# Five instead of four sets of single-row transfers per head, split between SyncE and ScalarE

## The reference

```python
kv_scores, indices = _pk(x, Wq_pk, pk_keys)          # top 16 of 128 x 128 keys, per token and head
ind = indices + offsets[None, None, :, None]         # a head has its own 16384 rows
k = jnp.einsum('bnhk,bnhkd->bnhd', kv_scores, keys_table[ind])
v = jnp.einsum('bnhk,bnhkd->bnhd', kv_scores, values_table[ind])
sim = jnp.where(causal, jnp.einsum('bihd,bjhd->bhij', q, k), neg)
out = jnp.einsum('bhij,bjhd->bhid', softmax(sim), v)
return out.transpose(0, 2, 1, 3).reshape(b, n, HEADS * DIM) @ Wo
```

## Time and profile before

| What | Value |
|---|---|
| Median of 3 runs | 10074.95 us (10071.83 to 10075.61) |
| Span of the profiled execution | 10059.9 us (its own time is not listed; the median of the runs is 15.05 us longer than the span) |
| POOL busy | 7544.0 us, 75% of the span |
| DVE, PE, ACT busy | 69%, 57%, 31% |
| Chain that ended last | POOL 73%, issue 24% |
| DMA, mean | 109 GB/s |
| Mean granted TensorE clock | 0.748 |

### The profile page before, as it was taken

How to read it: one execution, slowest core, us unless ns; L and a number is a source line. 1 busy time by engine, 2 the same in 40 slices (tenths; PEclk the granted TensorE clock), 3 DMA queues, 4 the chain that set the end, 5 groups by cost and what they waited for, 6 DMA issues and landing times.

```text
span 10059.9 us, 190416 instructions
## 1 busy us (share of the span) xinstructions
PE 5726.9 (57%) x23108; PEld 4551.2 (45%) x23108; DVE 6956.2 (69%) x42844; ACT 3087.9 (31%) x9770; POOL 7544.0 (75%) x7957
## 2 busy tenths in 40 slices
PE   5655555555555555555555555555555555555555
PEld 4544444444444444444444444444444444444444
DVE  8876667666666677676776666767667676666664
ACT  4333233233333333333333333333333332322222
POOL 5777777777777777777777777777777777777776
PEclk7877777777777777777777777777777777777777
DMA  3333343333433334333343333333333333333333
GB/s 109 105 109 109 109 114 109 109 109 109 113 109 109 109 109 113 109 109 109 109 113 109 109 109 109 113 109 109 109 111 111 110 109 109 109 111 109 109 109 100
DMA packets 503669, 1100.92 MB, mean 109 GB/s; under 512 B 196992, under 2 KB 246912, under 8 KB 502144
## 3 DMA queue, kind: packets, MB, share of 16 engines
q0 software_dynamic: 381120, 1041.22, 36.4%
q1 hardware_dynamic: 71488, 31.70, 1.3%
q10 hardware_dynamic: 49664, 16.42, 0.8%
HBM read 1084.36 MB, written 4.19 MB: 108 GB/s over the span
## 4 chain that ended last, share of the span: by engine, by line
POOL 73%; issue 24%; DVE 1%; PE 1%; POOLq 0%; DMA 0%; ACT 0%; ACTq 0%; SPq 0%; DVEq 0%
POOL ring L353 73%; DVE hot L1013 0%; DMA wo<-in_Wo 0%; POOLq L369 0%; PE ps_o L724 0%; ACTq L492 0%; POOLq L367 0%; DVE ps_v L935 0%; DMA ring<-in_table,idx 0%; PE ps_p L610 0%; PE ps_p L614 0%; DVE nmax L1064 0%; PE ps_s L748 0%; POOLq L368 0%; DVE cand L987 0%
## 5 line engine op out<-in xcount | busy, mean ns | idle before, releaser
L353 POOL DMA_INDIRECT ring<-in_table,idx x7940 | 7542.5, 950 | 2491.2 <-issue 2420.6
L671 PE MATMUL ps_w<-ring,diag 128*128 128x256 f32 x8192 | 2151.7, 423 | 13.0 <-issue 8.7
L715 PE MATMUL ps_p<-ident,prob 128*128 128x128 f32 x2304 | 564.7, 400 | 2304.0 <-ACT prob L453 2296.3
L671 PEld LDWEIGHTS ps_w<-ring,diag 128*128 128x128 f32 x8192 | 1740.6, 218 | 297.1 <-issue 19.7
L1013 DVE SCALAR_TENSOR_TENSOR hot<-rank,posf,cand 128x54 f32<-128x54 f32 x8192 | 1654.5, 271 | 0.3
L715 PEld LDWEIGHTS ps_p<-ident,prob 128*128 128x128 f32 x2304 | 395.1, 202 | 2501.0 <-ACT prob L453 1600.2
L932 DVE TENSOR_SCALAR ps_v<-ring,wgt 128x256 f32<-128x256 f32 x512 | 248.4, 485 | 1837.0 <-DMA ring<-in_table,idx 1836.8
L935 DVE SCALAR_TENSOR_TENSOR ps_v<-ring,wgt,ps_v 128x256 f32<-128x256 f32 x3072 | 1478.9, 481 | 19.6
L444 ACT ACTIVATE diag<-ident,wgt 128x128 f32<-128x128 f32 x4096 | 1251.8, 391 | 0.0
L453 ACT ACTIVATE prob<-ps_s,nmax 128x128 f32<-128x128 f32 (+7 forms) x512 | 378.1, 738 | 2300.8 <-issue 2259.6
L724 PEld LDWEIGHTS ps_o<-probT,kv 128*128 128x128 f32 x4608 | 986.7, 304 | 144.9 <-ACT probT L461 81.6
(11 more groups left out here) (119 smaller groups left out, 8141.2 us busy)
## 6 DMA issues: line engine op xcount, KB each, us to landing
far<-in_table SPq DMA_DIRECT2D x16352, 1.0 KB
far<-in_table ACTq DMA_DIRECT2D x15904, 1.0 KB
ring<-in_table,idx POOLq DMA_INDIRECT x7940
xin<-in_x SPq DMA_DIRECT2D x8, 512.0 KB
mask<-in_adj SPq DMA_DIRECT2D x1, 4096.0 KB, 15.9
out_x<-acc SPq DMA_DIRECT2D x64, 64.0 KB
far_row<-far_at SPq DMA_DIRECT2D x128, 0.5 KB
far_row<-far_at ACTq DMA_DIRECT2D x124, 0.5 KB
```

Of the source, the lines that this page charges most:

```text
L353: pool.indirect_dma_start(out=ring[:, t % RING, k, :], out_offset=None, in_=table, in_offset=bass.IndirectOffsetOnAxis(ap=idx[:, t, k:k + ...
L671: ins = nc.tensor.matmul(pw_ps, diag[:, k, :], ring[:, t % RING, k, :], start=(k == 0), stop=(k == PE_ROWS - 1))
L715: ins = nc.tensor.transpose(ps_p[:, c, (j % 4) * P:(j % 4 + 1) * P], prob[:, j * P:(j + 1) * P], ident[:])
```

## The change

There are five sets per head: t = 1, 6, 0, 4, 3 (`SETS`, in the order of their numbers 0 to 4). So POOL gathers 15 rows instead of 16 in five units per head from head 1 on. SP has the sets t = 1 and t = 6 whole and rows 0 to 95 of t = 3, 352 rows and 11 loads per head. ACT has t = 0 and t = 4 whole and rows 96 to 127 of t = 3, 288 rows per head. ACT's rows per unit are no longer 32 each: 40 in units 1, 2, 5 and 6 (two loads of 20), 48 in units 3 and 7 (two loads of 24), 16 in units 4 and 0 (one load of 16, of the shared set), 14 loads per head. The second load and its rows stand at the unit's end. The addresses of the shared set are turned into a row by SP (`far_begin`), and ACT waits for that in unit 4 (`near_load`, `waits`). In head 0 ACT now fetches too, in units 4 to 7. SP's order is t = 1, 3, 6, and in head 0 t = 0, 1, 3, 6. The load of a batch moves behind the first set of `turn`, and the stores stand before the last set.

```diff
-FAR = (3, 7)
-NEAR = (0, 4)
-SETS = FAR + NEAR
-NEAR_UNITS = 4
+SETS = (1, 6, 0, 4, 3)
+SP_ORDER = (0, 4, 1)
+SP_STOP = {0: P, 4: 96, 1: P}
+SP_FIRST_ORDER = (2, 0, 4, 1)
+NEAR_BEGIN = {1: 2, 5: 3}
+NEAR_PARTS = {1: (2, 0, (20, 20)), 2: (2, 40, (20, 20)), 3: (2, 80, (24, 24)), 4: (4, 96, (16,)),
+              5: (3, 0, (20, 20)), 6: (3, 40, (20, 20)), 7: (3, 80, (24, 24)), 0: (4, 112, (16,))}
+FIRST_PARTS = (4, 5, 6, 7)
...
-            def far_sets(n, sets, final=False):
-                for i in sets:
-                    if i < last_set:
-                        far_begin(n, i + 1)
-                    elif not final:
-                        far_begin(n + 1, 0)
+            def far_sets(n, order, follows):
+                for j, i in enumerate(order):
+                    if j + 1 < len(order):
+                        far_begin(n, order[j + 1])
+                    elif follows is not None:
+                        far_begin(n + 1, follows)
                     far_fetch(n, i)
...
-            def near_load(n, i, part):
-
-                if part in (0, NEAR_UNITS - 1):
+            def near_load(n, i, q, rows, waits):
+
+                if waits:
                     act.wait_ge(far_row_dma[i], n * 16)
...
-                    fetch = not first and (ahead or t == 0)
+                    fetch = t in FIRST_PARTS if first else ahead or t == 0
                     if fetch:
-                        near = len(FAR) + (t - 1) % UNITS // NEAR_UNITS
-                        part = (t - 1) % NEAR_UNITS
-                        at = near_load(n + 1 if t else n, near, part)
-                        near_rows(near, part, at, range(0, HIDDEN))
+                        near, start, loads = NEAR_PARTS[t]
+                        at = near_load(n + 1 if t else n, near, start, loads[0], True)
+                        near_rows(near, start, at[:HIDDEN])
...
                     if fetch:
-                        near_rows(near, part, at, range(HIDDEN, LOADED))
+                        near_rows(near, start + HIDDEN, at[HIDDEN:])
+                        start += loads[0]
+                        for rows in loads[1:]:
+                            near_rows(near, start, near_load(n + 1 if t else n, near, start, rows, False))
+                            start += rows
```

More of the change, by code:

```diff
@@ L279, in far_begin, with far_fetch @@
                     sp.dma_start(far_row[0:1, i, :], far_at[:, i:i + 1]).then_inc(far_row_dma[i], 16)
-            def far_fetch(n, i, stop=P):
+            def far_fetch(n, i):
                 sp.wait_ge(far_row_dma[i], n * 16)
@@ L287, in far_fetch @@
                     sp.sem_inc(sp_mark, 1)
-                for q in range(0, stop, LOADED):
+                for q in range(0, SP_STOP.get(i, P), LOADED):
                     _, at = nc.values_load_multi_w_load_instructions(
@@ L309, in turn @@
+            def turn(b, more):
+                n = (b + 1) * HEADS
+                far_begin(n, SP_ORDER[1])
+                far_fetch(n, SP_ORDER[0])
+                if more:
+                    load(b + 2)
+                far_begin(n, SP_ORDER[2])
+                far_fetch(n, SP_ORDER[1])
+                far_begin(n + 1, SP_ORDER[0])
                 stores(b)
-                far_sets((b + 1) * HEADS, range(last_set, last_set + 1))
+                far_fetch(n, SP_ORDER[2])
             load(1)
-            far_begin(1, last_set + 1)
@@ L314, in _ @@
[L314 to L321, removed]
+            far_begin(1, SP_FIRST_ORDER[0])
+            far_sets(1, SP_FIRST_ORDER, SP_ORDER[0])
             with sp.Fori(2, HEADS) as h:
-                far_sets(h, range(len(FAR)))
+                far_sets(h, SP_ORDER, SP_ORDER[0])
@@ L324, in _ @@
             with sp.Fori(0, BATCH - 2) as b:
-                load(b + 2)
-                turn(b)
+                turn(b, True)
                 with sp.Fori(1, HEADS) as h:
-                    far_sets((b + 1) * HEADS + h, range(len(FAR)))
-            turn(BATCH - 2)
+                    far_sets((b + 1) * HEADS + h, SP_ORDER, SP_ORDER[0])
+            turn(BATCH - 2, False)
             with sp.Fori(1, HEADS - 1) as h:
-                far_sets((BATCH - 1) * HEADS + h, range(len(FAR)))
-            far_sets(BATCH * HEADS - 1, range(len(FAR)), True)
+                far_sets((BATCH - 1) * HEADS + h, SP_ORDER, SP_ORDER[0])
@@ L333, in _ @@
+            far_sets(BATCH * HEADS - 1, SP_ORDER, None)
             stores(BATCH - 1)
@@ L473, in near_begin @@
                     act.dma_start(far_row[0:1, i, :], far_at[:, i:i + 1]).then_inc(far_row_dma[i], 16)
-            def near_load(n, i, part):
-                if part in (0, NEAR_UNITS - 1):
+            def near_load(n, i, q, rows, waits):
+                if waits:
                     act.wait_ge(far_row_dma[i], n * 16)
                     act.sem_inc(act_mark, 1)
-                    act.wait_ge(rows_summed, (n - 1) * UNITS + SETS[i] + 1)
-                    act.sem_inc(act_mark, 1)
-                q = part * LOADED
+                    if not (isinstance(n, int) and n == 1):
+                        act.wait_ge(rows_summed, (n - 1) * UNITS + SETS[i] + 1)
+                        act.sem_inc(act_mark, 1)
                 _, at = nc.values_load_multi_w_load_instructions(
-                    far_row[0:1, i, q:q + LOADED], engines=[mybir.EngineType.Activation],
+                    far_row[0:1, i, q:q + rows], engines=[mybir.EngineType.Activation],
                     min_val=0, max_val=(HEADS * NUM_KV - 1) * KV_BYTES,
@@ L487, in near_load, with near_rows @@
                 return at
[L489 to L492, removed]
+            def near_rows(i, q, at):
+                for j, offset in enumerate(at):
+                    act.dma_start(far[q + j:q + j + 1, i, :].bitcast(U8), table_bytes[bass.ds(offset, KV_BYTES)]) \
                         .then_inc(far_dma[i], 16)
@@ L537, in head @@
                         graph_keep(b + 1, h, g)
-                    if ahead and t in (1, 1 + NEAR_UNITS) and not first:
-                        near_begin(n + 1, len(FAR) + t // NEAR_UNITS)
+                    if ahead and t in NEAR_BEGIN and not (first and t not in FIRST_PARTS):
+                        near_begin(n + 1, NEAR_BEGIN[t])
                     if ahead:
```

3 lines of the change are left out of this document (removed).

## The result

The changed kernel takes 10662.66 us (median of 4 runs, 10655.61 to 10667.38) against 10074.03 us beside it: 1.0583 times as long, 95% interval 1.0568 to 1.0598. The forecast was 10494 us with a range of 10260 to 10760, so the sign and the range were right and the value 169 us too low. The profiled execution has a span of 10653.8 us.

What follows compares the result with a forecast made beforehand. ACT's stream replaces POOL as the bound: first sum at 360, 55 heads at 160.5 (8828), batch starts 80, stores 29, seven heads 1081, last head 102; span 10480, median 10494 us, 4.2% slower, range 10260 to 10760.

Steps and rivals of the forecast that it cites:

- What bounds the kernel: POOL sets the pace at 155.6 us per head; ACT is next at 138.24, in head 2.
- The hand-over: ACT's unit 4 waits for addresses SP turns; ACT arrives 1.2 us after them, nothing counted; 4.1 us wait once per batch.
- Rival 3: SP's delivery of addresses binds instead of ACT's own work; 5% slower SP rows give 77 us, 10571; inside the range.
- The start: In head 0 ACT stalls 27 us before its unit 4 load; sum of (1, 0) at 360 instead of 301.2.
- The base: ACT's pace per head with 256 rows, before the change, taken from head 2: 138.24 us.
- The additions: What changed rows and loads add on ACT per head: 20.0 us with proportional loads, 29.6 with constant loads.
- a quarter of the way from 158.3 to 167.9: ACT's pace per head, chosen between proportional loads (158.3 us) and constant loads (167.9): 160.5 us.
- the range's lower end: 10260 us, an ACT pace of 156.2: proportional loads, rows at 0.306, a third of unit 0's saving kept.
- Rival 2: ACT's loads take 2.14 us whatever their size: 167.9 us per head, 10902 us; chance 0.08.
- The largest term: Unit 0's 16 fewer rows on ACT count nothing, because ACT waits there for DVE's next results.
- rival 1: POOL stays the bound and the kernel is faster: 10047 us, about 9996 if the start is covered; chance 0.10.
- The signs named ahead: Among them: `wq_cur` every 160 us, POOL waiting some 350 us for sums, DVE hardly waiting for rows, shorter kT/ew waits.

## Why the prediction was right, and what it mis-sized

**What bounds the kernel.** Right in each step. POOL was the bound, one gather less is worth 79 us (79.8 measured), and ACT's stream stood 16 us behind it. That ACT shows as 31% busy says nothing, because the page doesn't count its transfers and loads.

**The hand-over.** The mechanism was right, the margin smaller: in ordinary heads the addresses came 0.4 us ahead of `kT` in the mean, where ACT was forecast to arrive 1.2 us after them. Rival 3 would have decided had ACT been faster, as the run without second loads shows. The wait behind the stores came once per batch, 2.3 to 3.5 us instead of 4.1, some 20 us in all instead of 29.

**The start.** 360 forecast, 354.62 measured, the stall 27.7 us (from `kT`'s end at 246.4 to the load at 274.1) instead of 27, from the same cause.

**The sum.** From the sum of (56, 0) back to that of (8, 0) are 7943.3 us. 48 heads at 163.9 make 7866, which leaves 77 for the six batch starts in them; with the first start they come to 90. In batch 0 a head takes 162.3. So the 55 heads are 174 us longer than at 160.5, and the batch starts with the stores 19 us shorter than the 109 forecast. From (56, 0) to (63, 0) are 1101.9 us instead of 1081, since ACT, at about 158 per head, is the bound there too, not POOL; in heads 57 to 61 its load of unit 4 starts 1.2 to 1.7 us after `kT`, so there it also waits for SP's addresses. After that it took 104.7 instead of 102. With 5 us less at the start: 174 - 19 + 21 + 3 - 5 = 174, the difference of the spans, 10653.8 and 10480. The median lies 8.9 us above the span, not 15.05.

**The step that was mis-sized is ACT's pace**, 160.5 against 163.9, in two terms. The base: head 2 was chosen because POOL doesn't disturb it, but it belongs to batch 0, and the later heads of the same stream take 139.7, 1.5 us more. The earlier trace rows had shown 4.3 us from the last row to `wq_cur` in head 30, a hint that was used for the batch starts alone. The additions: 24.1 us (163.87 - 139.74) against 22.3 taken. With the measured loads in the forecast's own formula they are 21.9. That formula credits 4.7 us for shorter first loads (4 x 0.70 + 2 x 0.46 + 0.94). In the traces the ninth row starts only 2.6 us earlier in units 1 to 7 together, so 2.1 us are not earned, and 21.9 + 2.1 is 24.0. Unit by unit, the changed kernel less the layout of before with twelve gathers: units 1, 2, 5 and 6 add 4.2, 4.5, 3.8 and 3.7 us, units 3 and 7 add 7.1 and 7.0, unit 4 gives back 6.3, and unit 0 stays as it is. Two slips of the working changed little: a quarter of the way from 158.3 to 167.9 is 160.7, not 160.5, and the conditions of the range's lower end give a pace of about 155.6, not 156.2.

**The size of a load** was a little nearer to proportion than I took. The Trainium skill ("DMA: Bandwidth & Descriptors", section "Latency and other measured facts") gives a floor of about 600 ns. Taken as a price at zero addresses, as the forecast took it, the trace doesn't agree: the line through 1.20, 1.48, 1.72 and 2.14 us meets zero at about 0.25. Taken as a least duration, no run shows it: the shortest load here took 1.18 us. Rival 2, loads of one price, is out.

**The largest term** was one set at zero. The 16 rows taken out of unit 0 earned nothing, as forecast, since ACT waits there for DVE and PE: the unit takes 17.3 us with 16 rows as with 32. The forecast treated this as a detail of the sum. It is the larger part of the loss: laid out evenly, the same 288 rows take 152.6 us, and what rival 1 describes (POOL stays the bound, "10047, or about 9996") happens, at 10019 and 10012. Of the 11.3 us between 152.6 and 163.9 some 4 are four more loads at 1.0; the other 7 fit the 8.6 us of waits in unit 0, of which the layout of before has 2.5 and the even one next to nothing. Neither cure alone was enough: without second loads a head still took 158.6, and with even rows but 18 loads 160.5. The signs named ahead were all seen (`wq_cur` at 163.8, POOL waiting for sums, DVE no longer waiting for rows, ACT waiting less for `kT` and `ew`). What no sign named is that ACT waits ten times as long for `nmax` (40.5 us in the kernel before, 420.0 now).

## What to carry to other kernels

Before work is moved to an engine, take its pace from a stretch where the present bound is absent, and take that stretch from the steady state, not from the start. Price each unit of its stream apart: work taken out of a unit that waits for other engines earns nothing, and the same work added to a full unit costs in full, so an uneven share can lose more than the whole change is worth. When one wait is removed, ask by how much the next was hidden; here it was 0.4 us.

## What the runs showed of the hardware that was not expected

A register load on ACT took about 0.25 us and 0.06 us per address (1.20 us for 16, 2.14 for 32). Splitting a load of 32 cost 1.0 us, twice what the durations and the slower first row behind it explain (0.5), because the first load runs beside other work and of the 0.94 us by which it became shorter only 0.57 arrived behind `qT`.

The small DMA that turns 128 addresses landed after 2.1 us in most places, and after 6.9 us where ACT started it directly behind 40 single transfers. That these hold it up is a guess; it was not tried apart.
